# Two sums of state products moved from GpSimd and VectorE to accumulating DMAs, with the last add of softplus on VectorE, in a fused Mamba block on one core

## The reference

```python
delta = softplus(dt @ Wdt.T + dt_bias)              # D = 2048 channels
dA = exp(d_t[..., None] * A)                        # N = 16 states per channel
state = dA * state + (d_t * u_t)[..., None] * B_t[:, None, :]
y_t = einsum('bdn,bn->bd', state, C_t)              # the sum over 16 states
y = (y + u * D_param) * silu(gate)
```

## Time and profile before

| | us |
|---|---|
| median of three runs | 2444.64 |
| the profiled execution, its own time | 2442.7 |
| its span | 2440.9 |
| PE busy | 2240.2 (92%) |
| DVE busy | 2229.0 (91%) |
| POOL busy | 2116.4 (87%) |
| ACT busy | 1614.2 (66%) |
| DMA engines busy, mean | 4 to 5 tenths |

### The profile page before, as it was taken

One profiled execution on the slowest core, in us unless ns is written; L12 is line 12 of the kernel. 1 busy time (PEld: TensorE's weight loads), 2 busy tenths in 40 slices (PEclk: granted clock), 3 DMA queues, 4 the chain that ended last, 5 costly groups with the idle time before them and its releaser, 6 DMA issues.

```text
span 2440.9 us, 30553 instructions
## 1 busy us (share of the span) xinstructions
PE 2240.2 (92%) x10140; PEld 1900.0 (78%) x10140; DVE 2229.0 (91%) x2104; ACT 1614.2 (66%) x3763; POOL 2116.4 (87%) x1090
## 2 busy tenths in 40 slices
PE   8989999999899998999989999999989977787879
PEld 7777878888678877888868887788878765666767
DVE  1389999999999999999999999999999999998892
ACT  1467667776777667776677667776677666765550
POOL 0189889999999999999899999999899999999870
PEclk9999999999999999999989998999999998989989
DMA  7454445444454444544455433644345332632342
GB/s 227 143 202 109 139 137 172 150 138 132 125 191 154 147 139 158 165 147 139 136 168 161 148 130 118 208 159 136 117 165 161 122 108 70 202 104 96 112 139 97
DMA packets 133178, 352.15 MB, mean 144 GB/s; under 512 B 38733, under 2 KB 43341, under 8 KB 131549
## 3 DMA queue, kind: packets, MB, share of 16 engines
q1 hardware_dynamic: 110254, 298.28, 37.9%
q10 hardware_dynamic: 22768, 51.93, 6.2%
HBM read 339.14 MB, written 11.02 MB: 143 GB/s over the span
## 4 chain that ended last, share of the span: by engine, by line
PE 42%; POOL 22%; DVE 21%; issue 9%; ACT 6%; DMA 1%; ACTq 0%; SPq 0%; DVEq 0%; POOLq 0%
POOL st L1530 12%; DVE scan L1303 11%; PE late L692 8%; PE ubank L638 7%; PE ubank L611 7%; POOL st L1538 6%; PE gbank L590 3%; DVE st L1315 3%; DVE ubank L1284 2%; PE scan L611 2%; DVE scan L1313 2%; ACT L1223 2%; POOL st L1544 2%; ACT scan L1133 2%; PE gbank L655 2%
## 5 line engine op out<-in xcount | busy, mean ns | idle before, releaser
L1530 POOL TENSOR_TENSOR st<-w_sb,bc 128x1024 f32<-128x1024 f32 x512 | 1198.0, 2357 | 122.7 <-PE gbank L655 110.3
L1303 DVE TENSOR_TENSOR_SCAN scan<-scan,st 128x1024 f32<-128x1024 f32 x512 | 1167.5, 2288 | 33.9 <-ACT scan L1133 18.4
L1133 ACT ACTIVATE scan<-delta,A_sb 128x255 f32<-128x255 f32 x2048 | 846.1, 459 | 0.1
L1538 POOL TENSOR_TENSOR st<-st 128x1024 f32<-128x1024 f32 x255 | 601.1, 2357 | 20.8 <-DVE st L1315 10.8
L611 PE MATMUL ubank<-h,wt 128*128 128x256 f32 x1712 | 423.3, 404 | 93.1 <-ACT qg L1223 87.6
L638 PE MATMUL ubank<-h,wt 128*128 128x256 f32 x2048 | 471.2, 384 | 23.2 <-ACT qg L1223 23.2
L611 PEld LDWEIGHTS ubank<-h,wt 128*128 128x128 f32 x1712 | 345.2, 204 | 161.8 <-ACT qg L1223 109.2
L638 PEld LDWEIGHTS ubank<-h,wt 128*128 128x128 f32 x2048 | 393.6, 193 | 81.7 <-ACT qg L1223 27.2
L1315 DVE TENSOR_TENSOR st<-scan,bc 128x1024 f32<-128x1024 f32 x384 | 453.8, 1208 | 0.0
L692 PE MATMUL late<-yg,wt 128*128 128x256 f32 x1792 | 407.1, 386 | 26.3 <-DVE x L1340 22.1
L1130 ACT ACTIVATE scan<-iota 128x4 f32<-128x4 f32 x512 | 86.9, 170 | 491.7 <-DVE st L1315 455.9
(11 more groups left out here) (219 smaller groups left out, 2257.1 us busy)
## 6 DMA issues: line engine op xcount, KB each, us to landing
wt<-in_W_in SPq DMA_DIRECT2D x256, 512.0 KB, 3.6
wt<-in_W_out SPq DMA_DIRECT2D x132, 512.0 KB, 3.4
wt<-in_cond_W SPq DMA_DIRECT2D x64, 512.0 KB, 3.6
bc<-bc_rows ACTq DMA_DIRECT2D x64, 512.0 KB, 6.8
wt<-G_tiles SPq DMA_DIRECT2D x32, 512.0 KB, 3.6
wt<-in_ffn_B SPq DMA_DIRECT2D x20, 512.0 KB, 3.6
xb<-in_x SPq DMA_DIRECT2D x8, 1024.0 KB, 7.1
x<-in_x ACTq DMA_DIRECT2D x28, 256.0 KB, 4.0
```

The costliest lines, as they stand in the source:

```text
L1133: last = fn(t[:, k, 1:T], delta[:, c, 1:T], ACT.Exp, scale=A_sb[:, col:col + 1])
L1303: v_.tensor_tensor_scan(Tps[q % 2][:, :], Tps[q % 2][:, :], x_, 0.0, ALU.mult, ALU.add).then_inc(scan_done, 1)
L1530: tt(st[:, n % ST_RING, :, :], w_sb[:, i % 2:i % 2 + 1, :].to_broadcast([P, NQ, T]), bc[:, 0, q * NQ:(q + 1) * NQ, :], ALU.mult).then_inc( ...
L1538: tt(st[:, n % ST_RING, :, :], st[:, n % ST_RING, :, :], st[:, (n - 1) % ST_RING, :, :], ALU.add).then_inc(add_done, 1)
```

## The change

What it does:

- **Sums of products.** All four quarters are now multiplied into their planes by DVE. `add_first` is gone. A DMA issued by POOL with an add on its destination makes q1 += q0 (`add_dma(i, 1)`); POOL adds q1 to q2 (`add`, once per slot); a second DMA makes q3 += q2 (`add_dma(i, 3)`); POOL folds q3 one slot later (`fold(i - 1)`), and PE sums as before.
- **Ring.** `st` has eight planes. `tmp`, `wT` and `sel` give their room: `wT` now lies in `la`, and `weights_b` takes columns of `ident`, two narrow matmuls where one stood.
- **Softplus.** ACT takes |x| straight into `delta`, then exp and log there (the relu evacuation is gone); DVE ends it with one instruction, max(x, 0) + delta, reading x in PSUM (`delta_sum`), where POOL's `delta_add` stood.
- **DVE's order in a slot.** scan 0, product 0, scan 1, product 1, scan 2, taps, scan 3, products 2 and 3 (before: scan 0, scan 1, product 0, product 1, `add_first`, scan 2, taps, scan 3, products 2 and 3).
- **PE's table.** The two `cond` chunks 2 and 3 leave slots 7 and 8's half place for the small place of slots 6 and 8, and each is begun one slot earlier with half of its matmuls. The adapter `la` and `cond` chunks 0 and 1 of batch b + 3 move to slots 13 to 15, and `Bs` 4 to 7 to slots 0 to 3.
- **Loads.** SP loads the next batch's input ahead of slot 12's tiles (before: slot 13's). ACT loads B from slot 14 on (before: slot 15), and spreads the x2 loads and the stores.

```diff
-ST_RING = 6
+ST_RING = 8
...
-    if c == 9 and j < B:
-        return ("cond", j, 4)
+    if c in (6, 8, 9) and j < B:
+        return ("cond", j, {6: 2, 8: 3, 9: 4}[c])
...
+def small_begun(i):
+    b, c = split(i)
+    return small_job(i + 1) if b and c in (5, 7) else None
...
-    if j < B and c in (3, 5, 7, 8, 9, 11):
-        return ("cond", j, {3: 0, 5: 1, 7: 2, 8: 3, 9: 5, 11: 7}[c])
-    if c == 14 and b + 3 < B:
-        return ("la", b + 3, 0)
-    if c == 15 and b < LAST:
-        return ("Bs", f, 4)
+    if j < B and c in (9, 11):
+        return ("cond", j, {9: 5, 11: 7}[c])
+    if c >= 13 and b + 3 < B:
+        return (("la", b + 3, 0), ("cond", b + 3, 0), ("cond", b + 3, 1))[c - 13]
...
-                if c == 13 and b + 3 < B:
+                if c == (13 if b == 0 else 12) and b + 3 < B:
                     sp.wait_ge(*made(("cond", b + 2, 7)))
...
-                return mm(o, sel[:, m * P:(m + 1) * P], wT[:, :], start=True, stop=True)
+                for e in range(2):
+                    pick = ident[0:E, 2 * m + e:2 * m + e + 1].to_broadcast([E, ER])
+                    last = mm(o[e * ER:(e + 1) * ER, :], pick, wT[:, :], start=True, stop=True)
...
+                fn(flat, home(("dt", b, j))[:, :], ACT.Abs).then_inc(sp_step, 1)
+                act.wait_ge(sp_step, 3 * n + 1)
                 fn(flat, flat, ACT.Exp, scale=-1.0).then_inc(sp_step, 1)
...
+            def delta_sum(b, j):
...
+                dve.wait_ge(sp_step, 3 * n + 3)
+                v_.scalar_tensor_tensor(d, home(job)[:, :], 0.0, d, ALU.max, ALU.add).then_inc(delta_done, 1)
+                dve.wait_ge(delta_done, n + 1)
+                dve.sem_inc(ev_inc(job), 1)
...
-                if q == 2 and i:
-                    pool.wait_ge(mul_done, 4 * i - 2)
-                if q == 1 and i >= 2:
+                if q == 3 and i >= 2:
                     pool.wait_ge(id_mm, i - 1)
...
+            def add_dma(i, k):
+                n = 4 * i + k
+                pool.wait_ge(mul_done, n + 1)
                 if k == 3:
-                    pool.wait_ge(add_done, 3 * i + 1)
+                    pool.wait_ge(add_done, 2 * i + 1)
+                pool.dma_start(st[:, n % ST_RING, :, :], st[:, (n - 1) % ST_RING, :, :], accum_op=ALU.add
+                               ).then_inc(acc_st[k // 2], 16)
...
+                if not last:
                     weight(i + 1)
+                    dbu(i + 1, 0)
+                    dbu(i + 1, 1)
+                if i:
+                    fold(i - 1)
+                add_dma(i, 1)
+                if not last:
+                    dbu(i + 1, 2)
                     dbu(i + 1, 3)
+                add(i)
+                if not last:
+                    add_dma(i, 3)
```

More of the change, by code:

```diff
@@ L191, in slot_tiles @@
     tiles = []
-    for job in (late_job(i), small_job(i), half_job(i)):
+    for job in (late_job(i), None if i and small_begun(i - 1) else small_job(i), small_begun(i), half_job(i)):
         if job:
@@ L376, in build @@
         scan_done = sem("scan_done")
-        prod_done = sem("prod_done")
         mul_done = sem("mul_done")
         add_done = sem("add_done")
+        acc_st = [sem(f"acc_st{i}") for i in range(2)]
         id_mm = sem("id_mm")
@@ L395, in build @@
         block = ctx.enter_context(nc.Block())
-        N_CONSTS = 12
+        N_CONSTS = 11
         SOFT_STEPS = 10
@@ L584, in adapter, with cond_begin, cond_chunk @@
                 last.then_inc(done_inc(job), 1)
-            def cond_chunk(o, j, m):
+            def cond_begin(o, j, m):
                 n = TILE_NO[("cond", j, m)]
                 pe.wait_ge(*loaded(n))
-                for k in range(KH):
+                for k in range(PAIRS):
+                    last = mm(o, wt[:, n % W_RING, k, :], xb[:, k, :], start=(k == 0), stop=False)
+                return last
+            def cond_chunk(o, j, m, first=0):
+                n = TILE_NO[("cond", j, m)]
+                pe.wait_ge(*loaded(n))
+                for k in range(first, KH):
                     mm(o, wt[:, n % W_RING, k, :], xb[:, k, :], start=(k == 0), stop=False)
@@ L778, in run @@
                         pe.wait_ge(*emptied(("la", b, 0)))
-                    cond_chunk(o[:, 0:T], b, k).then_inc(inc, 1)
+                    first = PAIRS if job in SMALL_NO and small_begun(i - 1) else 0
+                    cond_chunk(o[:, 0:T], b, k, first).then_inc(inc, 1)
                 elif kind == "xp":
@@ L1422, in _ @@
             norm(0)
+            delta_sum(0, 0)
+            delta_sum(0, 1)
             def take_late(i):
```

131 lines of the change are left out of this document (54 added, 77 removed).

## The result

The changed kernel takes **2473.6 us** (median of five, 2452.9 to 2475.8) against 2445.3 for the kernel before beside it: ratio 1.0097, 95% interval 1.0063 to 1.0131. It is slower by 1%, where 2380 and a gain were forecast; the stated range of 2352 to 2478 takes the time in only by its slow end. Its executions spread over 23 us, those of the kernel before over 3. The profiled one is the fastest of the five, so its trace explains only a part of the loss; what follows compares stretches of it.

The account below looks back on a forecast made before the run. It took DVE to bound blocks 1 to 5 and POOL block 7's slots 0 to 7. Terms -4 - 46 - 12 - 16 + 12 = -66 on 2442.7 gave 2377, stated as 2380 us, range 2352 to 2478.

Parts of the forecast that it names:

- about 4.5 us: Blocks 1 to 5: PE's lag by slot 13 delays DVE, taking the block from 267.8 to 272 us.
- Block 7: Last block: -16 us, as -12 in slots 0 to 7 and -4 in slots 9 to 13.
- Block 6: Block with no cond work left and no PE excess: -12 us from DVE's savings less its added costs.
- Block 0: First block: slots 6 to 10 stay PE's, the others win 1.1 or 0.3 us; -4 us.
- mean landing: Time from issue to landing of an adding DMA, L, taken as 5.7 us; 3.6 and 7.1 kept as ends.
- is hidden in a slot of 16.7 as long as L < 6.5: POOL's waits for the adding DMAs cost nothing while issue to landing, L, stays under 6.5 us.
- 2L + 3.7: POOL's turn: fold 1.27, add 2.35 and two landings of L each; 15.1 us at L = 5.7.
- Landings late +2 per block, +12: Slots 14 to 0, where B and C load too, and slot 12's wait for cond chunk 7: +12 us.
- 15.7 against 16.7: POOL's work per slot at 15.7 us, below DVE's 16.7, so POOL would not be the bound.
- x: POOL's time to issue one DMA, taken as 1 us, in its slot of 13.7 + 2x.
- issue is dear, x of 2 or more: Rival: POOL's DMA issue takes 2 us or more, every slot is 17.7, total 2475 us; chance 0.05.
- Landings set the slot: Rival: landings of 7.1 us make every slot of blocks 1 to 6 17.9, total 2485 us; chance 0.22.

Follow-up runs that it names:

- e10: Changed kernel with both adding DMAs moving 256 KB in place of 512, so values differ: 2402.1 us, ratio 0.9839.
- e12: Changed kernel loading only half of each u, gate, cond and output weight tile from tile 60 on, so values differ: 2404.0 us, ratio 0.9844.
- e13: Changed kernel with POOL's weight for the slot after next put ahead of the second adding DMA: 2449.6 us, ratio 1.0017.
- e8: Changed kernel with the two adding DMAs as plain copies of the same size, so values differ: 2396.3 us, ratio 0.9811.
- e1: Changed kernel with ACT's loads of B back at slot 15: 2498.7 us, ratio 1.0212.
- e6: Changed kernel, no cond chunk begun early, PE's half job ahead of the sums, ACT's loads of B later in slot 14: 2460.7 us, ratio 1.0084.
- e3: Changed kernel with ACT's loads of B back at slot 15 and no cond chunk begun a slot early: 2480.1 us, ratio 1.0146.
- e16: Changed kernel with POOL's weight ahead of the second adding DMA and no cond chunk begun a slot early: 2435.4 us, ratio 0.9967.
- e5: Changed kernel with no cond chunk begun early and PE's half job run ahead of the sums of the states: 2467.2 us, ratio 1.0085.
- e14: e16 with ACT's first two loads of B behind u's evacuation in slot 14 and PE's half job ahead of the sums in slot 9: 2434.3 us, 0.9970.

## Why the prediction was wrong

- **The work of DVE and PE was counted well over a block.** Block 3: DVE is busy for 265.6 us, PE for 268.8 (266.5 forecast). By slot PE's count was off: the narrow passes of `la` and `la2` were priced like the others, which gave slot 13 20.3 us where it has 17.5. The "about 4.5 us" per block that were to reach DVE, 22 in all, did not come that way.
- **Block 7 came out in sum, blocks 0 and 6 in part.** Block 7 lost 18 us (forecast 16), with some luck: its slots 0 to 7 lost 8 of 12, the rest 10 where 4 were forecast. Block 6 lost 6.6 of the 12, its slot 14 having grown from 15.7 to 19.4. Block 0, from its first `y_gate` on, grew by 0.3 where -4 was forecast, by slot 14 too; what lies ahead of that first `y_gate` is 3.0 us longer, which I did not follow.
- **The mean landing held, and was the wrong number.** 5.80 us in the mean against the 5.7 taken. The step that failed is the sentence that the turn "is hidden in a slot of 16.7 as long as L < 6.5". It is wrong on both sides. From slot 9's rows the turn is 2L + 4.3, not 2L + 3.7: from `fold` to the issue 1.21 us, from `add` to the next issue 2.98, and 0.07 twice from a landing to its reader. And the slots that have to hide it are not the mean slot but slots 6 to 8, of 16.0 us. So the limit is L < 5.8, which is the mean landing itself: 97 of 255 were over it, 45 over 7 us, up to 11.0. Not each of them costs, as slot 12 shows, but those in slots 6 to 8 can reach slots 7 to 9. The page of before would have given a hint: the same 512 KB took 3.6 us as a weight load and 6.8 as a broadcast, and I read this as two kinds of transfer, not as one engine pool under load. In the changed kernel, which spreads the broadcasts over more time, they land after 4.9.
- **"Landings late +2 per block, +12" was the mis-sized term.** By e10 and e12 either stream at half its size gives 70 us. The DMA share was forecast at 0.85; it is 0.76 in block 3, and that is a mean over bursts: 0.89 in the 10 us of the long landing.
- **POOL's turn had less slack than 15.7 against 16.7.** x was taken as 1; it is 0.9, and POOL's own wait, at nothing in the sum, adds 0.6. Measured: 0.60 us per issue until the next instruction starts, 0.3 more in that next one, and once 0.63 for POOL's own add: 16.1. DVE's slots 6 to 8 are 16.0. The rival "issue is dear, x of 2 or more" was not true as put, but half a microsecond decided: e13 gets 24 us for 0.6.
- **Who waits for `fold` was not followed to the end.** The prediction looked at POOL's own loop. `fold(i - 1)` now stands behind the next slot's weight and two products, PE's sums behind it, in slots 9 and 14 a cond chunk behind these, and then `y_sum`. In slot 9 PE has so little to do ahead of the sums that it comes early, and falls to the lower clock while it stands. The forecast looked for PE being late by its work; it was late by waiting.
- **Slot 14 was costed by its passes alone.** The adapter and cond work put there and ACT's loads of B make it 3 us longer per block than before, 20 us over blocks 0 to 6, and shorter landings don't change that (e8, e10, e12). Which part is whose stays open: e1 clears it in the blocks without that work, e6 in blocks 1, 3 and 4, and neither gains time.
- **The begun tile** was costed at nothing; it costs 14 to 19 us (e1 to e3, e13 to e16). **The earlier loads of B** were costed at nothing too: as against slot 15 they are worth 25 us with these DMAs (e1), though ACT stands before them.
- **The sign.** Two rivals lie near the measured 2473.6 in number, and neither in mechanism. "POOL's issue is dear" says 2475, but for slots of 17.7 throughout, and by the same sum over the blocks as its neighbour's these would give about 2463. "Landings set the slot" says 2485, for slots of 17.9 throughout. The slots are as short as forecast in most places and 3 to 11 us longer in one or two of each block.

## What to carry to other kernels

- For a wait on a DMA take the upper tenth of its landings (here 8 us and more) under the load that the change itself makes, not the mean (5.8). An adding DMA took the engines for twice the time of a copy; ask which other stream runs in bursts there.
- Follow a later step to the last reader. What counts is the slack at the tightest slot, here 16.1 us of POOL against 16.0 of DVE, and not against the mean slot; fill the time in which an in-order engine waits for its own result with the next independent instruction.
- A stall that is removed at one place shows nothing yet: e5 and e14 cleared slot 9 and gained no time.
